# Another order for the steps of the first two of four graph layers: low halves before maxima, joins and statistics

## The chip, the cores and the metric

The kernel runs on one core of a Trainium2 chip. The metric is the time of one execution on the device in microseconds (us), the median of several runs. The two kernels do the same operations on the same tiles; only their order in the engines' queues differs.

## The reference

Four graph layers over 1354 nodes with 256 features, each ahead of a residual sum. `adj` is a sparse weighted 1354 x 1354 matrix.

```python
h = relu(layernorm(x)); x = x + softmax(q k^T / 16 + adj + adj) v            # layer 0: q, k, v = h Wq^T + bq, ...
h = relu(layernorm(x)); x = x + sigmoid(attn_a * x_a + attn_b * x_b)         # layer 1
#   attn_a, attn_b = sigmoid([adj h, h] Wa^T + ba), the same with Wb, bb
#   e = where(adj != 0, exp(-leaky_relu(s_left + s_right^T, 0.01)), 0)
#   x_a = (e h W_sa) / (rowsum(e) + 1e-5);  x_b = adj (h W_gcnb) + b_gcnb
h = relu(layernorm(x)); x = x + (adj != 0) (h W + b) / deg                   # layer 2
h = relu(layernorm(x)); x = x + (S * softmax(mask(h' U h'^T))) h'            # layer 3: h' = h W, S = adj + I
```

## The kernel before

**Tiles.** The node dimension is cut into NB = 11 row blocks of 128 (the last has 74) and NG = 3 column groups: 512, 512 and 330 columns wide, that is 4, 4 and 3 blocks. A tile is one row block by one group, so NT = 33 tiles, n = 11 * group + row block. Tiles 10, 21 and 32 have 74 rows.

**Exactness.** Most products are made of a high and a low half of each operand: hi*hi + hi*lo + lo*hi. ScalarE (ACT) writes the high half, and VectorE (DVE) or GpSimd (POOL) subtracts it from the exact value for the low half. So every sum over a tile (`weighted`, L1508) runs hi matmuls at L1519 and L1520 for each of its blocks, then waits for the low half, then runs the lo matmuls at L1524.

**Order.** Each engine has one queue, whose order is written out by hand, in steps. Between engines there are semaphores only. A wait holds everything that stands behind it on its engine.

**Layer 0, second part** (step `s` from 11 on). TensorE (PE) at step s does `score(s)` (while s < 33) and `aggregate0(s - 15)`, which needs the two exponentials and the low half of tile s - 15. DVE at step s does `add(s)` (L890: scores plus adjacency), `shift(s - 13)` (L929: subtract the maximum), `running(s)` (L921: running maximum over a group) and `weights_lo(s - 14)` (L935: low half of the weights). `add(s)` also waits until `weights_lo(s - 15)` has freed its slot. ACT at step s does `exps(s - 13)`, two exponentials (L523 the high half, L524 the exact value, on which `weights_lo` waits), and up to step 30 one piece of the degree count. `add_out(gi)` (L943, L947) adds a finished group to x on DVE; the next group's first tile waits for it block by block. `top` (L899) turns the maximum of a group into a row: it waits for PE's `turn_max` (which waits for the last `running` of the group), and PE's `spread_max` waits for it. From step 36 on the head of layer 1 is mixed in: `turn(b, 1)` on PE (L1408), `h_full(b)` on ACT (L476), which evacuates it and frees the one bank that all turns use, and the projections `project_g(b)` and `project_h(b)` (L1438). The statistics of the normalisation (`stats` L843, `aggr` L848) are DVE's, and its power and product (`norm`, L376 and L379) are POOL's.

**Layer 1** (step `k` from LEAD = 8 on). PE at step k does `aggregate_b(k)` (adjacency sum, low half `adj_lo(k)`: DVE for even tiles at L1097, POOL for odd ones at L413) and `aggregate_a(k - 8)` (attention sum, low half `e_lo_part(k - 8)`, L1119). Where k is a multiple of 11 the two change places. DVE at step k does `e_lo_part(k - 7)`, a pair `mask` (L1104) and `ramp` (L1112) for a tile ahead of ACT's `exp1` (L643, L644), `adj_lo(k + 1)` where that is even, and once for each group `sums_b` (L1127), `gates`, `join` (L1145 to L1155), `add_gated` (L1163), `stats` and `aggr`. The first tile of a group's `aggregate_a` waits for `join` of the group before, block by block. `ramps_at(k)` (L55) says which ramps stand in a step: one, but two at steps 22 and 27. At steps 14 to 18 DVE also makes masks of layer 2 (`mask_2`, L1174). At steps 34 and 38 PE makes a product of weights (L1415), the second of them after ACT's copy `gram` (L734). ACT's z2 and h2_hi (L482, L490) normalise for layer 2.

## Time and profile before

| | us |
|---|---|
| median of 3 runs | 411.68 |
| the three runs | 411.44, 991.74, 411.68 |
| the profiled execution, its own time | 410.53 |
| its span, from first to last instruction | 408.7 |

The profile is of the execution with 410.53 us, 1.83 us of which lie outside the span. Times of instructions below count from the start of the span. An instruction's row shows when it starts and how long it takes; the next one on an engine may start before it has ended, so the distance of two starts is what a queue pays, and the duration is what a waiter pays. TensorE's granted clock is 0.995 of 2.4 GHz in the mean.

### The profile page before, as it was taken

How to read it: one execution, taken by the hardware profiler on the slowest of the kernel's cores; microseconds unless marked ns; L12 is line 12 of the kernel's file. 1: busy time of each engine (PE TensorE's matmuls, PEld its weight loads, DVE VectorE, ACT ScalarE, POOL GpSimd, SP SyncE). 2: the span in 40 equal slices, each digit the busy share in tenths (PEclk: the TensorE clock that was granted, in tenths of full speed). 3: DMA queues.
4: the chain of work that ended last, by engine and by line, in shares of the span. 5: the costliest groups of instructions: out<-in, count | busy, mean ns of one | idle time of the engine just before them, and what ended most of it. 6: DMA issues, size and time to landing. Idle time of an engine off the chain costs nothing.

```text
span 408.7 us, 7331 instructions
## 1 busy us (share of the span) xinstructions
PE 391.2 (96%) x2526; PEld 353.1 (86%) x2526; DVE 327.6 (80%) x751; ACT 222.7 (54%) x466; POOL 89.7 (22%) x105
## 2 busy tenths in 40 slices
PE   8999999999899999999989999999998999999995
PEld 6788888988899899999989899988887788889863
DVE  6898898899874856998998988765739688798763
ACT  3453798988785657876777891255331312212320
POOL 1290000002010514331130101051010133334552
PEclk9999999999999999999999999999999999999998
DMA  7994000000000001000000000000000000010011
GB/s 233 383 379 142 0 0 2 2 0 2 0 2 0 2 2 51 2 2 0 3 2 0 3 0 2 0 2 2 0 2 0 2 1 0 2 51 2 0 53 33
DMA packets 10317, 13.96 MB, mean 34 GB/s; under 512 B 661, under 2 KB 7209, under 8 KB 10281
## 3 DMA queue, kind: packets, MB, share of 16 engines
q1 hardware_dynamic: 9736, 12.96, 9.3%
q10 hardware_dynamic: 544, 0.52, 0.4%
q8 instruction: 21, 0.34, 0.3%
q14 instruction: 16, 0.12, 0.1%
HBM read 12.10 MB, written 1.39 MB: 33 GB/s over the span
## 4 chain that ended last, share of the span: by engine, by line
PE 77%; DVE 13%; issue 6%; ACT 1%; POOL 1%; DVEq 0%; POOLq 0%; ACTq 0%
PE ps L1805 9%; PE ps L1524 9%; PE ps L1519 8%; PE ps L1520 8%; PE ps L309 8%; PE ps L311 8%; PE ps L310 8%; PE ps L1438 4%; PE ps L1731 3%; PE ps L1732 3%; PE ps L1761 2%; PE ps L1408 2%; DVE m_sb L921 1%; DVE p_lo L935 1%; DVE s_sb L929 1%
## 5 line engine op out<-in xcount | busy, mean ns | idle before, releaser
L1519 PE MATMUL ps<-v_hi,p_hi 128*128 128x258 f32 (+3 forms) x242 | 64.4, 296 | 0.9 <-DVE x_sb L947 0.7
L1520 PE MATMUL ps<-v_lo,p_hi 128*128 128x258 f32 (+3 forms) x242 | 61.1, 281 | 0.0
L1805 PE MATMUL ps<-v,w_ring 128*128 128x256 f32 (+3 forms) x242 | 58.0, 385 | 1.3 <-DVE w_ring L1337 0.8
L1805 PEld LDWEIGHTS ps<-v,w_ring 128*128 128x128 f32 (+3 forms) x242 | 43.2, 186 | 11.0 <-DVE w_ring L1337 4.5
L376 POOL TENSOR_TENSOR mr_all<-mr_all,mhalf 128x4 f32<-128x4 f32 (+1 forms) x12 | 13.3, 1106 | 168.5 <-DVE mr_all L853 168.5
L1519 PEld LDWEIGHTS ps<-v_hi,p_hi 128*128 128x128 f32 (+3 forms) x242 | 44.6, 184 | 2.9 <-ACT p_hi L523 0.9
L814 ACT ACTIVATE s_sb<-s_sb 128x512 f32<-128x512 f32 (+3 forms) x30 | 17.3, 576 | 53.9 <-DVE s_sb L929 53.9
L1520 PEld LDWEIGHTS ps<-v_lo,p_hi 128*128 128x128 f32 (+3 forms) x242 | 44.7, 185 | 0.6
L453 POOL TENSOR_TENSOR total<-total,s_sb 128x512 f32<-128x512 f32 (+3 forms) x27 | 30.6, 1134 | 65.1 <-DVE w_ring L1337 65.1
L1524 PE MATMUL ps<-v_hi,p_lo 128*128 128x258 f32 (+3 forms) x242 | 40.4, 285 | 2.9 <-DVE p_lo L935 2.5
L929 DVE TENSOR_TENSOR s_sb<-s_sb,ps 128x512 f32<-128x512 f32 (+3 forms) x63 | 38.5, 612 | 0.8 <-PE ps L1506 0.7
L1524 PEld LDWEIGHTS ps<-v_hi,p_lo 128*128 128x128 f32 (+3 forms) x242 | 32.5, 185 | 4.3 <-DVE p_lo L935 3.4
L921 DVE TENSOR_TENSOR m_sb<-m_sb,s_sb 128x512 f32<-128x512 f32 (+3 forms) x51 | 33.6, 658 | 0.9
L413 POOL TENSOR_TENSOR mid_lo<-adjT_sb,mid_hi 128x512 fp32r<-128x512 f32 (+2 forms) x16 | 20.6, 1289 | 51.4 <-ACT mid_hi L634 51.4
L1519 PE MATMUL ps<-big_hi,mid_hi 128*128 128x258 f32 (+3 forms) x121 | 31.7, 293 | 0.0
L1520 PE MATMUL ps<-big_lo,mid_hi 128*128 128x258 f32 (+3 forms) x121 | 30.3, 282 | 0.0
L309 PE MATMUL ps<-mid_hi,v_hi 128*128 128x512 f32 (+3 forms) x66 | 28.5, 432 | 1.0 <-DVE v_lo L859 1.0
L643 ACT ACTIVATE p_hi<-s_sb,minus_r 128x512 fp32r<-128x512 f32 (+3 forms) x33 | 22.2, 672 | 11.2 <-PE ps L1524 4.5
L1112 DVE SCALAR_TENSOR_TENSOR s_sb<-s_sb,sx 128x512 f32<-128x512 f32 (+3 forms) x33 | 26.1, 790 | 1.2
L1329 DVE SCALAR_TENSOR_TENSOR s_sb<-adjT_sb,ps 128x512 f32<-128x512 f32 (+3 forms) x30 | 18.5, 616 | 10.0 <-PE ps L311 9.9
L309 PE MATMUL ps<-mid_hi,big_hi 128*128 128x512 f32 (+3 forms) x66 | 25.4, 385 | 0.6 <-DVE mid_lo L872 0.6
L1337 DVE TENSOR_TENSOR w_ring<-s_sb,adjT_sb 128x512 f32<-128x512 f32 (+3 forms) x30 | 19.4, 648 | 7.1 <-ACT s_sb L814 7.1
(228 smaller groups left out, 1045.0 us busy)
## 6 DMA issues: line engine op xcount, KB each, us to landing
adjT_sb<-in_adjT_dram SPq DMA_DIRECT2D x1, 2816.0 KB, 16.7
adjT_sb<-in_adjT_dram SPq DMA_DIRECT2D x3, 768.0 KB, 9.1
adjT_sb<-in_adjT_dram SPq DMA_DIRECT2D x1, 1815.0 KB, 21.2
out_dram<-x_sb SPq DMA_DIRECT2D x10, 128.0 KB
x_sb<-in_x_dram SPq DMA_DIRECT2D x2, 256.0 KB, 3.6
x_sb<-in_x_dram SPq DMA_DIRECT2D x1, 512.0 KB, 4.6
adjT_sb<-in_adjT_dram SPq DMA_DIRECT2D x1, 512.0 KB, 11.4
rows_sb<-in_rows_dram SPq DMA_DIRECT2D x1, 385.0 KB, 11.1
```

The costliest lines, as they stand in the source:

```text
L309: eng.matmul(out_ap, lhs[0], rhs[0], start=first, stop=False)
L310: eng.matmul(out_ap, lhs[0], rhs[1], start=False, stop=False)
L311: return eng.matmul(out_ap, lhs[1], rhs[0], start=False, stop=last)
L453: pool.tensor_tensor(r, r, slot3(n), ALU.add).then_inc(tot_add, 1)
L643: act.activation(ring(p_hi, n), sum1(n), ACT.Exp, bias=bias, scale=SLOPE - 1.0).then_inc(e_hi, 1)
L921: dve.tensor_tensor(m, m, mine(n), op).then_inc(s_max[a], 1)
L929: dve.tensor_tensor(mine(n), mine(n), ps[0:rows(j), bank, 0:CW[gi]], ALU.subtract).then_inc(s_sub[a], 1)
L1112: dve.scalar_tensor_tensor(out=sum1(n), in0=left[0:rows(j), gi, 0:CW[gi]], scalar=sx[0:rows(j), j, 0:1], in1=sum1(n), op0=ALU.add, op1=ALU ...
L1519: pe.matmul(out_ap, left_[0][0:k, n % RING, mine], right_[0][0:k, j, 0:cols_], start=(j == 0), stop=False)
L1520: pe.matmul(out_ap, left_[0][0:k, n % RING, mine], right_[1][0:k, j, 0:cols_], start=False, stop=False)
L1524: ins = pe.matmul(ps[0:rows(b), banks[b % PER], 0:cols_], left_[1][0:k, n % RING, mine], right_[0][0:k, j, 0:cols_], start=False, stop=(j ...
L1805: ins = pe.matmul(ps[0:rows(b), SUMS3[gi][b % PER], 0:D], w_ring[0:k, n % RING, mine], v3[0:k, j, :], start=(j == 0), stop=(j == NB - 1))
```

## The change

All edits are of order.

1. **Layer 0, DVE, steps 14 to 30:** `weights_lo` goes ahead of `add_out` and `running`, and at step 14 ahead of `shift` too.
2. **Layer 0, DVE, steps 31 to 46:** `weights_lo(s - 14)`, then `shift(s - 13)`, now stand before `add(s)`, `add_out` and `running`. The reciprocal of the degrees goes from step 36 to 40.
3. **Layer 0, PE and ACT:** `turn(0, 1)` stands before `aggregate0(21)`, `project_g(0)` before `aggregate0(22)` (it was after `aggregate0(23)`), and ACT's `h_full(0)` a step earlier.
4. **Layer 1, POOL:** `adj_lo(1)` goes ahead of `norm(1, 2)`; `norm(2, 1)` a step later.
5. **Layer 1, DVE:** the double ramp of step 22 goes to step 12, so ramps 8 to 17 come one step sooner. `adj_lo(k + 1)` goes ahead of `join`, `e_lo_part` and the ramps. `add_gated`, `stats` and `aggr` of the first two groups are spread over four steps, two blocks a step.
6. **Layer 1, PE:** `aggregate_b(31)` goes from step 31 to step 30, between `aggregate_b(30)` and `aggregate_a(22)`.

```diff
 def ramps_at(k):
-    first = k - LEAD + 3 + (k > 22) + (k > 27)
-    return range(first, min(first + (2 if k in (22, 27) else 1), NT))
+    first = k - LEAD + 3 + (k > 12) + (k > 27)
+    return range(first, min(first + (2 if k in (12, 27) else 1), NT))
...
             sides(0)
+            adj_lo(1)
             norm(1, 2)
-            adj_lo(1)
             sides(1)
...
-                if k == 35:
+                if k == 36:
                     norm(2, 1)
...
-                if 36 <= s < 40:
+                if s == 35:
+                    h_full(0)
+                if 37 <= s < 40:
                     h_full(s - 36)
...
+                late = s >= NT - 2
+                if late:
+                    weights_lo(s - 14)
+                    if s < NT + 13:
+                        shift(s - 13, 0)
                 if s < NT:
                     add(s)
-                if 13 <= s < NT + 13:
+                if s == 14:
+                    weights_lo(0)
+                if not late and s >= 13:
                     shift(s - 13, 0)
+                if 14 < s < NT - 2:
+                    weights_lo(s - 14)
                 for gi in range(2):
                     if s == NB * gi + 25:
                         add_out(gi)
                 if s < NT:
                     running(s, 0, ALU.max)
-                if s >= 14:
-                    weights_lo(s - 14)
-                if s == 36:
+                if s == 40:
                     dve.wait_ge(nz_sum, NB)
...
                 for gi in range(NG):
                     if k == NB * gi + 11:
                         sums_b(gi)
-                    if gi < 2 and k == NB * gi + 19:
+                if k + 1 < NT and (k + 1) % 2 == 0:
+                    adj_lo(k + 1)
+                for gi in range(2):
+                    if k == NB * gi + 19:
                         join(gi)
                 if m + 1 < NT:
                     e_lo_part(m + 1)
                 for n in ramps_at(k):
                     mask(n)
                     ramp(n)
-                if k + 1 < NT and (k + 1) % 2 == 0:
-                    adj_lo(k + 1)
...
-                    if gi < 2 and k == NB * gi + 21:
-                        add_gated(gi)
-                    if gi < 2 and k == NB * gi + 22:
-                        for b in blocks(gi):
-                            stats(b, 2)
-                    if gi < 2 and k == NB * gi + 23:
-                        for b in blocks(gi):
-                            aggr(b, 2)
+                for gi in range(2):
+                    b0, step = blocks(gi)[0], k - NB * gi - 21
+                    if step in (0, 1):
+                        add_gated(b0 + 2 * step)
+                        add_gated(b0 + 2 * step + 1)
+                    if step in (1, 2):
+                        stats(b0 + 2 * step - 2, 2)
+                        stats(b0 + 2 * step - 1, 2)
+                    if step in (2, 3):
+                        aggr(b0 + 2 * step - 4, 2)
+                        aggr(b0 + 2 * step - 3, 2)
...
+                if s == 36:
+                    pe.wait_ge(s_sub[0], 2 * NB)
+                    turn(0, 1)
+                if s == 37:
+                    project_g(0)
                 if s >= LAG:
                     aggregate0(s - LAG)
...
-                if s == 36:
-                    pe.wait_ge(s_sub[0], 2 * NB)
-                if 36 <= s < 40:
+                if 37 <= s < 40:
                     turn(s - 36, 1)
-                if 38 <= s < 42:
+                if 39 <= s < 42:
                     project_g(s - 38)
...
-                if k < NT and k % NB:
+                if k < NT and k % NB and k != 31:
                     aggregate_b(k)
+                if k == 30:
+                    aggregate_b(31)
                 aggregate_a(k - LEAD)
```

`add_gated` now takes a block in place of a group; the last group's call loops over its blocks.

## Rows read from the trace of the kernel before

**Rows 1.** The page, busy time of each engine over the span.

```profile
PE 391.2 (96%) x2526; PEld 353.1 (86%) x2526; DVE 327.6 (80%) x751; ACT 222.7 (54%) x466; POOL 89.7 (22%) x105
```

**Rows 2.** Windows: stretch, its length, each engine's busy us, clock, DMA.

```profile
100.00:110.00 10.00, 8.37 (x66) 7.65 (x64) 8.77 (x20) 7.17 (x15) 2.23 (x2) 1.00 0.00 1
...
230.00:240.00 10.00, 9.39 (x63) 8.28 (x63) 8.11 (x31) 10.00 (x24) 1.42 (x2) 1.00 0.01 3
```

**Rows 3.** Waits of PE over the span: total us, times, longest.

```profile
PE ps L1524 <- DVE p_lo L935: 2.5, 4, 1.0
...
PE ps L1524 <- DVE p_lo L1119: 0.4, 2, 0.2
```

**Rows 4.** Timeline, step 14 of layer 0: start, duration, engine, line.

```profile
52.02 0.62 ACT L524 ACTIVATE s_sb<-s_sb 128x512 f32<-128x512 f32 x1
...
52.57 0.68 DVE L929 TENSOR_TENSOR s_sb<-s_sb,ps 128x512 f32<-128x512 f32 x1
...
53.77 0.69 DVE L935 TENSOR_TENSOR p_lo<-s_sb,p_hi 128x512 fp32r<-128x512 f32 x1
...
54.51 0.76 PE L1524 MATMUL ps<-v_hi,p_lo 128*128 128x258 f32 x4 [0.72 <-DVE p_lo L935]
```

**Rows 5.** Timeline, step 25 of layer 0.

```profile
82.82 1.66 DVE L947 SCALAR_TENSOR_TENSOR x_sb<-ps,rinv,x_sb 128x256 f32<-128x256 f32 x4
...
84.39 0.49 DVE L921 TENSOR_TENSOR m_sb<-m_sb,s_sb 128x330 f32<-128x330 f32 x1
...
85.54 0.76 PE L1524 MATMUL ps<-v_hi,p_lo 128*128 128x258 f32 x4 [0.50 <-DVE p_lo L935]
```

**Rows 6.** Timeline, steps 32 to 37 of layer 0.

```profile
102.18 0.67 DVE L929 TENSOR_TENSOR s_sb<-s_sb,ps 128x512 f32<-128x512 f32 x1
...
102.31 0.75 PE L1524 MATMUL ps<-v_hi,p_lo 128*128 128x258 f32 x4 [0.96 <-DVE p_lo L935]
...
103.43 0.61 ACT L524 ACTIVATE s_sb<-s_sb 128x512 f32<-128x512 f32 x1
...
104.20 0.64 PE L1524 MATMUL ps<-v_hi,p_lo 128*128 128x258 f32 x4
...
108.06 0.18 DVE L943 RECIPROCAL rinv<-ps 128x4 f32<-128x4 f32 x1 [0.77 <-PE ps L1524]
108.17 0.46 ACT L524 ACTIVATE s_sb<-s_sb 128x330 f32<-128x330 f32 x1
...
108.92 0.36 PE L1519 MATMUL ps<-v_hi,p_hi 128*128 128x258 f32 x1 [0.67 <-DVE x_sb L947]
```

**Rows 7.** Timeline, start of layer 1's sums.

```profile
137.68 1.55 POOL L376 TENSOR_TENSOR mr_all<-mr_all,mhalf 128x3 f32<-128x3 f32 x1 [4.29 <-DVE mr_all L853]
...
140.00 1.53 POOL L413 TENSOR_TENSOR mid_lo<-adjT_sb,mid_hi 128x512 fp32r<-128x512 f32 x1
...
141.58 0.75 PE L1524 MATMUL ps<-big_hi,mid_lo 128*128 128x258 f32 x4 [0.96 <-POOL mid_lo L413]
...
142.17 0.38 PE L1408 MATMUL ps<-ident,z_buf 128*128 128x128 f32 x2
```

**Rows 8.** Timeline, steps 8 to 30 of layer 1.

```profile
157.62 0.42 DVE L1104 TENSOR_SCALAR s_sb<-adjT_sb 128x512 f32<-128x512 f32 x1
...
160.59 1.29 POOL L413 TENSOR_TENSOR mid_lo<-adjT_sb,mid_hi 128x512 fp32r<-128x512 f32 x1 [0.81 <-ACT mid_hi L634]
...
160.63 1.54 DVE L1104 TENSOR_SCALAR s_sb<-adjT_sb 128x512 f32<-128x512 f32 x1
...
188.76 0.16 DVE L1145 TENSOR_TENSOR rs<-ps,e_left 128x4 f32<-128x4 f32 x1 [0.98 <-PE ps L1524]
...
193.41 0.74 PE L1524 MATMUL ps<-big_hi,mid_lo 128*128 128x258 f32 x4 [0.38 <-DVE mid_lo L1097]
...
205.59 0.62 PE L1524 MATMUL ps<-big_hi,mid_lo 128*128 128x258 f32 x3 [1.41 <-DVE mid_lo L1097]
...
221.59 0.36 PE L1519 MATMUL ps<-v_hi,p_hi 128*128 128x258 f32 x1 [0.21 <-DVE s_sb L1155]
```

More of the change, by code:

```diff
@@ L1156, in join, with add_gated @@
                                              op1=ALU.add).then_inc(joined, 1)
-            def add_gated(gi):
-                for b in blocks(gi):
-                    r = rows(b)
-                    dve.wait_ge(th_set, b + 1)
-                    dve.scalar_tensor_tensor(out=x_sb[0:r, b, :], in0=t2[0:r, gi % 2, b % PER, :], scalar=0.5,
-                                             in1=x_sb[0:r, b, :], op0=ALU.mult, op1=ALU.add).then_inc(x_add[1], 1)
+            def add_gated(b):
+                r, gi = rows(b), b // PER
+                dve.wait_ge(th_set, b + 1)
+                dve.scalar_tensor_tensor(out=x_sb[0:r, b, :], in0=t2[0:r, gi % 2, b % PER, :], scalar=0.5,
+                                         in1=x_sb[0:r, b, :], op0=ALU.mult, op1=ALU.add).then_inc(x_add[1], 1)
             def mask_2(n):
@@ L1238, in _ @@
                         gates(gi)
-                    if gi < 2 and k == NB * gi + 21:
-                        add_gated(gi)
-                    if gi < 2 and k == NB * gi + 22:
-                        for b in blocks(gi):
-                            stats(b, 2)
-                    if gi < 2 and k == NB * gi + 23:
-                        for b in blocks(gi):
-                            aggr(b, 2)
+                for gi in range(2):
[9 more added lines that the diff above has]
+                        aggr(b0 + 2 * step - 3, 2)
                 if 14 <= k < 19:
@@ L1285, in _ @@
                 mask_2(n)
-            add_gated(2)
+            for b in blocks(2):
+                add_gated(b)
             for b in blocks(2):
```

## The prediction

> **What bounds the kernel now.** I read the page's busy times first. PE works 391.2 of 408.7 us [rows 1], so an edit of order can give back only what PE waits. Then the waits of PE by releaser: nearly all inside the first two layers are waits of a sum's lo matmuls (L1524) for a low half on another engine, 2.5 us for `weights_lo` and 0.4 for `e_lo_part` [rows 3], and single ones for `adj_lo`, the longest 1.41 [rows 8]. Then the windows: the worst stretch is 100 to 110, the end of layer 0, with PE at 8.37 of 10 and DVE at 8.77, while 230 to 240, the end of layer 1, has PE at 9.39 and ACT at 10.00 [rows 2]. Last the timeline at each wait [rows 4 to 8], for what stood on the late engine ahead of the thing waited for. No queue of DMA is in any of these chains.
>
> **Layer 0, step 14.** The exact value of tile 0 is there at 52.64 (52.02 + 0.62). DVE does `shift(1)` at 52.57, a `running` after it, and `weights_lo(0)` only at 53.77: two operations at 0.60 each ahead of it. PE starts the lo matmuls at 54.51 after 0.72 idle [rows 4]. In the new order `weights_lo(0)` starts at about 52.70 and ends at 53.39, before PE wants it, and the restart costs PE another 0.1 (its group takes 0.76 where an undelayed one takes 0.64 [rows 4, 6]). Saved: 1.0 with the end of the previous matmul counted in. `shift(1)` is 0.7 later, but PE needs its tile two us after that. Bounds: 0.7 to 1.0.
>
> **Layer 0, step 25.** Four `add_out` operations start at 82.82 and take 1.66, `running` follows at 84.39, `weights_lo(11)` behind it, and PE stands until 85.54 after 0.50 idle [rows 5]. With `weights_lo(11)` first, it ends before `add_out` starts. `add_out` itself then comes 0.24 later relative to PE, because the low half takes 0.60 of a 0.36 us gap, and PE's hi matmuls follow it block by block. Saved: 0.50 + 0.1 of restart + 0.2 of end overlap, less 0.24, about 0.55. Bounds 0.3 to 0.8.
>
> **Layer 0, steps 31 to 46: here I expect a loss.** At step 32 the new order cures the longest wait for a `weights_lo`, 0.96 at 102.31 [rows 6]. But `weights_lo(n)` ahead of `shift(n + 1)` joins two engines in one chain: `shift(n)` 0.67, two exponentials until 1.19 after the shift's end (shift at 102.18 + 0.67 = 102.85, second exponential ends at 103.43 + 0.61 = 104.04 [rows 6]), `weights_lo(n)` at 0.60, then the next shift. That is 0.67 + 1.19 + 0.04 + 0.60 = 2.50 a tile. Before, `shift(n + 1)` went out while ACT still worked on tile n, and the pair cost DVE 1.2. PE needs 12 matmuls at 0.12, that is 1.43, for a tile of the second group (0.12 is from the undelayed group of four at 104.20: 0.64 less 0.28, over 3). Nothing else stands in DVE's steps 33 and 35 to fill the gap. From the two-operation chain of step 32 I count on, in the present clock less the 1.5 gained so far:
> - `running(32)` is now behind `weights_lo`, `shift` and `add`: `turn_max` waits 0.7, `spread_max` 0.6.
> - `weights_lo` of tiles 19, 20 and 21 go out 2.5 apart: the sum of tile 21 waits 0.4 for its hi and 0.3 for its lo half.
> - `add_out(1)` starts 0.7 later than the present 108.06, at 108.8. PE meets `project_g(0)`, whose `h_full(0)` stands on ACT behind the exponentials of tile 22: 1.4 of wait.
> - `turn(2)` and `turn(3)` need one bank that `h_full` frees, behind exponentials that come later: 0.4 and 0.5.
>
> Together 4.3 of waits in place of the present 0.96 + 0.67 [rows 6] + 0.7 in three short ones around tile 22, which is 2.3: a loss of 2.0. From step 39 on each step has 0.9 us of projection in it, PE's step is about 2.0, and the chain for a 330-wide tile (0.41 + 0.5 + 0.83 + waits, the two exponentials from 0.37 and 0.46 [rows 6]) is about 1.9, so nothing more is lost. Moving `turn(0)` and `project_g(0)` puts 0.25 and 0.7 us of PE work into these waits; without it the loss would be larger by as much. Bounds: a gain of 1.6, if all the old waits go and none comes, to a loss of 6, if steps 39 to 46 lose 0.5 each.
>
> **Layer 1, POOL.** `norm(1, 2)` takes POOL from 137.68 to 140.00, `adj_lo(1)` ends at 141.53, PE stands 0.96 and turns block 8 at 142.17 [rows 7]. The new `adj_lo(1)` can start at 137.1 and ends by 138.6 at the latest. `norm` then ends 0.5 to 1.0 after the present 140.00, and z(8) with it, so the turn is what is late next: it comes at 141.4 to 141.7 where it would be free at 140.94. Saved 0.7; bounds 0.4 and 1.2.
>
> **Layer 1, steps 12 to 22.** The extra `mask` and `ramp` cost DVE 1.12 at step 12. The one long idle of DVE that can take it is the 0.98 before `join(0)` [rows 8]; small ones on the way I put at 0.5 together. `adj_lo(20)`, now ahead of `join(0)`, wants 0.60 of the same 0.98. So `join(0)` comes up to 0.5 late, and the sum behind it too, while PE's wait of 0.38 before 193.41 for `adj_lo(20)` [rows 8] goes, with 0.1 of restart. Net 0.2 saved, bounds from a loss of 0.6 to a gain of 0.6.
>
> **Layer 1, steps 22 to 24.** PE stands 1.41 before 205.59 for `adj_lo(24)` [rows 8], behind two ramp pairs, four gated sums and four statistics. Of these one ramp pair (1.12), two gated sums and two statistics go elsewhere, and `adj_lo` moves ahead of `e_lo_part` and a ramp (1.7). It can then start near 201.3 and PE wants it at 204.2. Saved: 1.41 + 0.1 = 1.5; bounds 1.0 and 1.5.
>
> **Layer 1, steps 30 to 37.** `aggregate_b(31)` fills the wait for `join(1)`: 0.21 [rows 8], 0.1 of restart and 0.2 of pacing block by block, 0.5. Its own low half has been ready for 4 us. The two waits for `e_lo_part` (0.4, [rows 3]) lose most of their cause: 0.3. Bounds 0.2 and 1.1 for both.
>
> **Rules weighed.** A mask of DVE takes 1.54 at 160.63, beside POOL's subtraction of 160.59 [rows 8]; alone, at 157.62, it takes 0.42 [rows 8]. The Trainium skill says why (SBUF — State Buffer, section "Who interferes with whom"): DVE and GpSimd share a pair of ports as an exclusive lock for a whole instruction. By that rule the extra mask of step 12 may meet a POOL subtraction, which is rival R5 below; the trace agrees with it at 160.63.
>
> **The sum.** -1.0 - 0.55 + 2.0 - 0.7 - 0.2 - 1.5 - 0.5 - 0.3 = -2.75. On the profiled execution, 410.53, that gives 407.8. The median of the runs shown is 1.15 above that execution, so the same difference gives 408.9 against 411.68. A measurement of this kernel can tell about 2%, or 8 us, from no change.
>
> **The rivals** (times on the median's scale).
> - *R1, the late steps cost nothing.* For it: ACT is busy only 7.17 of 10 in that stretch [rows 2] and PE has other work moved in. Against: a semaphore chain doesn't care how busy its engines are. 408.9 - 2.0 = 406.9.
> - *R2, the late steps gain all they can.* The 1.6 instead of the loss of 2.0: 405.3.
> - *R3, layer 1's gains are given back.* ACT is full from 230 to 240 [rows 2]. If its work, not its start, sets the end of layer 1, the 2.5 us of steps 12 to 37 go: 411.4. Against: its stretch starts with `sums_b(2)`, which also comes earlier.
> - *R4, slower.* The chain of `shift`, exponentials and `weights_lo` doesn't end at step 38 but also sets steps 39 to 46, because ACT has `h_full`, `h1_hi` and `z` in its queue between two tiles. Eight steps at 0.5 are 4.0 more: 412.9. It decides from the point at which the chain is longer than PE's step of 2.0; my 1.9 is close below.
> - *R5, the shared operands.* The mask and ramp of step 12 meet POOL's subtraction and take 1.1 more, `join(0)` is 1.0 later still and PE with it: 409.9.
> - *R6, no effect.* Freed waits reappear at once behind the same DVE, which is full for most of both layers: 411.7.
>
> **Chances.** Forecast 0.42, R1 0.19, R2 0.05, R3 0.14, R4 0.08, R5 0.06, R6 0.06. The forecast's own range is 407.4 to 410.4; with the rivals and the bounds 405.4 to 412.3. No case reaches 8 us either way, so within 2% has 0.95; PE's whole idle is 408.7 - 391.2 = 17.5 us [rows 1], of which start, end and two more layers take a share; so faster by over 2% has 0.03 and slower 0.02.
>
> **What would show it.** Right: no PE wait near 54 and 85; the long one at 102 gone, but new ones at `spread_max`, at `project_g(0)` and at the turns after it; `weights_lo` operations of tiles 19 to 21 about 2.5 apart; no PE wait of 1.4 for `adj_lo(24)`; a wait of about 0.5 before the turn of block 8. From the start of score step 31 to the first sum of layer 1 PE takes about 2 us more than now, and from there to 240 about 3 less. Wrong: if PE passes the end of layer 0 sooner by more than 1 us, the chain wasn't binding; if PE waits at steps 39 to 46, R4; if the second layer is no shorter, R3 or R6.

## The result, and the profile after

The changed kernel takes 409.7 us (median of 9 runs, 409.23 to 410.7), the kernel before, run beside it, 411.65. The ratio is 0.9971 with a 95% interval of 0.9958 to 0.9983: 1.2 us less (0.7 to 1.7), where 2.75 were predicted. The two medians lie 1.95 apart; the ratio leaves out two of the nine executions of the kernel before, of 646.73 and 991.74 us. The time is inside the predicted range, the size of the effect is not what was worked out.

The profiled execution took 410.70 us against 410.53 before, 0.17 more. Its first `add` of layer 0 starts at 18.78, before at 17.66. That is 1.12 us more of start-up, ahead of all that was changed, and the start varies between 17.65 and 18.71 in the experiments below. So I compare from that `add` on. Call L the time from it to the last group of lo matmuls of layer 1's sums: 222.67 us before (17.66 to 240.33), 221.73 after (18.78 to 240.51), 0.94 less. Each kernel has one trace. Where two kernels do the same, the distances between groups of matmuls mostly repeat to 0.02 us, so L can be read stretch by stretch. Three places repeat less well: the end of layer 0 when the clock falls there (0.1), the third tile of layer 1 (0.08), and the group of `adj_lo(26)` (up to 0.3, see E12).

The windows of the changed kernel that answer to [rows 2], with six single microseconds between them (stretch, length, busy us of PE, PEld, DVE, ACT and POOL, PE's granted clock, DMA):

```profile
100.00:110.00 10.00, 7.71 (x58) 6.64 (x56) 7.13 (x15) 6.04 (x12) 0.78 (x2) 1.00 0.00 1
230.00:240.00 10.00, 8.91 (x61) 8.02 (x60) 8.53 (x33) 9.81 (x23) 1.44 (x2) 1.00 0.01 3
109.00:110.00 1.00, 0.05 (x1) 0.05 (x1) 0.82 (x2) 0.90 (x3) 0.00 (x0) 1.00 0.00 0
110.00:111.00 1.00, 1.00 (x3) 0.83 (x4) 0.96 (x4) 0.88 (x3) 0.00 (x0) 0.61 0.00 0
111.00:112.00 1.00, 1.00 (x4) 0.81 (x4) 1.00 (x4) 0.46 (x1) 0.00 (x0) 0.50 0.00 0
112.00:113.00 1.00, 1.00 (x7) 1.00 (x6) 1.00 (x4) 0.28 (x1) 0.00 (x0) 0.50 0.00 0
113.00:114.00 1.00, 1.00 (x8) 1.00 (x8) 1.00 (x4) 0.57 (x2) 0.00 (x0) 0.69 0.00 0
114.00:115.00 1.00, 1.00 (x11) 1.00 (x11) 1.00 (x7) 0.94 (x3) 0.00 (x0) 1.00 0.00 0
```

The end of layer 0 has become worse (PE 7.71 of 10, it was 8.37), and after a microsecond with next to nothing on PE its clock goes from 2.4 to 1.2 GHz and is back at 1.00 only from 114 on. The end of layer 1 is worse too (8.91, it was 9.39; the windows are fixed in time and this trace starts 1.12 later, so they don't hold quite the same work).

The waits of PE by line, the five largest behind that `add` and inside the first two layers (in all, times, longest; one of the two for `m_sb`, of 0.2, lies in a later layer):

```profile
PE ps L1451 <- ACT h_mid L476: 1.3, 1, 1.3
PE ps L1532 <- DVE s_sb L1164: 1.2, 1, 1.2
PE ps L1537 <- DVE p_lo L1128: 1.1, 2, 0.6
PE ps L1510 <- DVE m_sb L923: 0.6, 2, 0.4
PE ps L1519 <- DVE mx L909: 0.4, 1, 0.4
```

L1451 is `project_g`, L1532 the hi matmuls behind `join`, L1537 the lo matmuls, L1510 and L1519 `turn_max` and `spread_max`. The 2.5 us for `weights_lo` of [rows 3] are gone altogether. Of these five, those of `project_g` and `spread_max` are new. The wait behind `join` was 0.2 (behind `join(1)`), those for `e_lo_part` 0.4, and `turn_max` had none in these layers and now has 0.43.

**The two cured waits.** The timeline at step 14 and step 25, DVE then PE:

```profile
53.80 0.69 DVE L937 TENSOR_TENSOR p_lo<-s_sb,p_hi 128x512 fp32r<-128x512 f32 x1
54.41 0.68 DVE L931 TENSOR_TENSOR s_sb<-s_sb,ps 128x512 f32<-128x512 f32 x1
54.77 0.64 PE L1537 MATMUL ps<-v_hi,p_lo 128*128 128x258 f32 x4
...
82.46 0.68 DVE L937 TENSOR_TENSOR p_lo<-s_sb,p_hi 128x512 fp32r<-128x512 f32 x1
83.27 1.66 DVE L949 SCALAR_TENSOR_TENSOR x_sb<-ps,rinv,x_sb 128x256 f32<-128x256 f32 x4
```

The low half now goes ahead of the shift and of `add_out`, and the PE row at 54.77 has no bracket, so no wait. Against [rows 4, 5] PE is 0.91 and 0.55 sooner at the groups that follow, once the 1.12 are taken off. At step 25 a wait of 0.21 stays, for `add_out`, as worked out (0.24).

**The chain at the end of layer 0.** The timeline of DVE's low halves and of PE there:

```profile
102.16 0.69 DVE L937 TENSOR_TENSOR p_lo<-s_sb,p_hi 128x512 fp32r<-128x512 f32 x1 [0.28 <-ACT s_sb L524]
104.66 0.69 DVE L937 TENSOR_TENSOR p_lo<-s_sb,p_hi 128x512 fp32r<-128x512 f32 x1 [0.35 <-ACT s_sb L524]
107.17 0.69 DVE L937 TENSOR_TENSOR p_lo<-s_sb,p_hi 74x512 fp32r<-74x512 f32 x1 [1.22 <-ACT s_sb L524]
109.95 1.87 PE L1451 MATMUL ps<-raw_b,h_mid 128*128 128x258 f32 x4 [1.30 <-ACT h_mid L476]
```

The low halves are 2.50 us apart, as worked out, each after DVE sat idle until ScalarE's second exponential (the brackets), and `project_g(0)` waits 1.30 (1.4 predicted).

**Around `join(0)`.** POOL, DVE and PE:

```profile
189.56 1.28 POOL L413 TENSOR_TENSOR mid_lo<-adjT_sb,mid_hi 75x512 fp32r<-75x512 f32 x1 [4.21 <-ACT mid_hi L636]
189.59 1.52 DVE L1182 TENSOR_SCALAR spare_mask<-adjT_sb 128x512 fp32r<-128x512 f32 x1
191.04 0.68 DVE L1106 TENSOR_TENSOR mid_lo<-adjT_sb,mid_hi 128x512 fp32r<-128x512 f32 x1
191.64 0.15 DVE L1154 TENSOR_TENSOR rs<-ps,e_left 128x4 f32<-128x4 f32 x1
192.87 0.36 PE L1532 MATMUL ps<-v_hi,p_hi 128*128 128x258 f32 x1 [1.16 <-DVE s_sb L1164]
```

A mask of 0.42 takes 1.52 beside POOL's subtraction for tile 21, `adj_lo(20)` follows, and only then `join(0)` begins. Before, DVE had 0.98 of idle there [rows 8]. That idle is gone.

The steps of the prediction against the two traces (distance between groups of lo matmuls, after less before):

| term | predicted | measured |
|---|---|---|
| layer 0, step 14 | -1.0 | -0.91 |
| layer 0, step 25 | -0.55 | -0.55 |
| layer 0, steps 31 to 46 | +2.0 | +2.17 |
| layer 1, POOL's order | -0.7 | -0.33 |
| layer 1, steps 12 to 22 (`join(0)`) | -0.2 | +0.70 |
| layer 1, steps 22 to 24 (`adj_lo(24)`) | -1.5 | -1.67 |
| layer 1, steps 30 to 37 | -0.5 - 0.3 | -0.31 |
| sum | -2.75 | -0.90, of L's -0.94 |

### The profile page after: what moved, and what is told of

The parts are those of the page before. It is cut to its first block, busy times and chain, and to the rows that moved or that the text cites. A ratio compares the mean times of both kernels' runs of the same rounds, so it can differ in the third digit from the quotient of the medians.

```text
span 408.9 us, 7331 instructions
## 1 busy us (share of the span) xinstructions
PE 393.3 (96%) x2526; PEld 355.2 (87%) x2526; DVE 329.8 (81%) x751; ACT 222.4 (54%) x466; POOL 90.1 (22%) x105
## 4 chain that ended last, share of the span: by engine, by line
PE 80%; DVE 11%; issue 5%; ACT 2%; DVEq 0%; POOLq 0%; POOL 0%; ACTq 0%
PE ps L1823 9%; PE ps L309 8%; PE ps L311 8%; PE ps L310 8%; PE ps L1532 8%; PE ps L1537 8%; PE ps L1533 8%; PE ps L1451 4%; PE ps L1750 3%; PE ps L1749 3%; PE ps L1779 2%; PE ps L1421 2%; DVE p_lo L1128 2%; DVE s_sb L931 1%; PE ps L1556 1%
## 5 line engine op out<-in xcount | busy, mean ns | idle before, releaser
L1532 PE MATMUL ps<-v_hi,p_hi 128*128 128x258 f32 (+3 forms) x242 | 64.7, 298 | 1.5 <-DVE s_sb L1164 1.2
L1532 PEld LDWEIGHTS ps<-v_hi,p_hi 128*128 128x128 f32 (+3 forms) x242 | 45.0, 186 | 3.3 <-issue 1.8
L1537 PE MATMUL ps<-v_hi,p_lo 128*128 128x258 f32 (+3 forms) x242 | 40.5, 285 | 1.1 <-DVE p_lo L1128 1.1
L1537 PEld LDWEIGHTS ps<-v_hi,p_lo 128*128 128x128 f32 (+3 forms) x242 | 32.8, 186 | 1.8 <-DVE p_lo L1128 1.6
L1532 PE MATMUL ps<-big_hi,mid_hi 128*128 128x258 f32 (+3 forms) x121 | 31.7, 293 | 0.0
L937 DVE TENSOR_TENSOR p_lo<-s_sb,p_hi 128x512 fp32r<-128x512 f32 (+3 forms) x33 | 20.6, 623 | 6.2 <-ACT s_sb L524 5.9
```

What stands on the lines that cost most here:

```text
L1532: pe.matmul(out_ap, left_[0][0:k, n % RING, mine], right_[0][0:k, j, 0:cols_], start=(j == 0), stop=False)
L1537: ins = pe.matmul(ps[0:rows(b), banks[b % PER], 0:cols_], left_[1][0:k, n % RING, mine], right_[0][0:k, j, 0:cols_], start=False, stop=(j ...
```

## The experiments

Each kernel was timed beside the kernel before. E1 to E4, E5 to E8 and E9 to E12 ran together, with a median of before of 411.05, 411.35 and 411.0, where it was 411.65 beside the changed kernel. So medians from different groups can differ by some tenths for no reason of the kernels. There the ratios, each to its own kernel before, are the better measure, and for small effects L. L is as above.

| run | median us | ratio to before, 95% | L |
|---|---|---|---|
| changed kernel | 409.7 | 0.9971 (0.9958, 0.9983) | 221.73 |
| E1 late order off | 406.5 | 0.9897 (0.988, 0.9913) | 218.35 |
| E2 mask behind join | 409.95 | 0.9969 (0.9959, 0.998) | 221.20 |
| E3 group 2 whole | 410.42 | 0.9988 (0.9977, 0.9999) | 221.96 |
| E4 PE kept busy | 409.35 | 0.9967 (0.9954, 0.9979) | 221.33 |
| E5 PE's and ACT's moves back | 411.76 | 1.0009 (0.9997, 1.0021) | 223.28 |
| E6 E1 and E5 together | 406.44 | 0.9882 (0.9867, 0.9898) | 218.53 |
| E7 E1, ramp back at 22 | 405.26 | 0.9856 (0.9842, 0.987) | 216.95 |
| E8 E1, POOL's order back | 407.04 | 0.99 (0.9886, 0.9914) | 218.75 |
| E9 E1, small subtraction | 405.9 | 0.9872 (0.9856, 0.9887) | 217.45 |
| E10 E1, join first | 406.48 | 0.9892 (0.9877, 0.9906) | 218.23 |
| E11 before, steps 14 to 30 alone | 409.41 | 0.9957 (0.9941, 0.9973) | 220.98 |
| E12 E7, aggregates later | 405.69 | 0.9866 (0.9848, 0.9884) | 217.21 |

**E1: the late order off.**

```diff
-                late = s >= NT - 2
+                late = False
...
-                if not late and s >= 13:
+                if 13 <= s < NT + 13:
                     shift(s - 13, 0)
-                if 14 < s < NT - 2:
+                if 14 < s:
                     weights_lo(s - 14)
```

> The changed kernel with only VectorE's order of steps 31 to 46 put back (shift before weights_lo; the moved turn and projection of TensorE, the moved h_full of ScalarE and all of the rest stay). Theory (the chain weights_lo, shift, two exponentials, 2.5 us a tile, is what costs): the stretch from score step 31 to the first sum of layer 1 is 1.5 to 2.5 us shorter than in the changed kernel, the old wait of about 1 us for a low half near 101 is back, the granted clock stays at 1.00 in 110 to 114; about 407.7 against 409.7. Rival (the moved turn and projection, or h_full a step earlier, cost the time): no shorter by more than 0.5 us, the clock still falls.

3.2 us less by the medians (3.0 by the ratios), 3.38 in L, nearly all of it (3.31) between step 31 and the end of layer 0. The theory holds and the size is larger than the bound given: the old wait doesn't come back as 1 us but as 0.27, since `weights_lo` still stands ahead of `running`. E1's windows:

```profile
100.00:110.00 10.00, 9.60 (x73) 8.87 (x73) 9.38 (x22) 8.08 (x18) 0.62 (x1) 1.00 0.00 0
110.00:120.00 10.00, 9.79 (x67) 8.83 (x66) 8.50 (x27) 8.69 (x25) 1.44 (x2) 1.00 0.01 2
```

**E5 and E6: the moved turn, projection and `h_full` put back,** with the late order (E5) and without it (E6).

```diff
-                if s == 35:
-                    h_full(0)
-                if 37 <= s < 40:
+                if 36 <= s < 40:
...
-                if s == 36:
-                    pe.wait_ge(s_sub[0], 2 * NB)
-                    turn(0, 1)
-                if s == 37:
-                    project_g(0)
...
-                if 37 <= s < 40:
+                if s == 36:
+                    pe.wait_ge(s_sub[0], 2 * NB)
+                if 36 <= s < 40:
                     turn(s - 36, 1)
-                if 39 <= s < 42:
+                if 38 <= s < 42:
                     project_g(s - 38)
```

> The changed kernel with the moved turn(0), project_g(0) and h_full(0) put back in their old steps; VectorE's late order stays. Theory of the prediction (the moved work fills waits that the chain of 2.5 us a tile makes): without it the end of layer 0 is 0.5 to 0.9 us longer, about 410.4. Rival (project_g(0) comes where its h_full isn't done, stands 1.3 us and brings the clock down, and that is what costs): the stretch is 0.5 us or more shorter and the clock stays at 1.00 in 110 to 114; about 409.0 or less.

> As the kernel with VectorE's late order undone (406.5), with turn(0), project_g(0) and h_full(0) put back too. Where the late order alone costs the 3.3 us, this one is within 0.5 us of 406.5, a little slower since the move fills the wait at spread_max: about 406.9. Rival (the order and the move are only bad together): it is as fast as 406.5 and the kernel with the move alone undone is as fast too.

E5 is 2.1 us slower than the changed kernel by the medians (1.6 by the ratios, 1.55 in L), E6 the same as E1. So the move is worth nothing by itself and about 1.6 us under the late order. The rival falls: PE without the moved work waits longer, 1.97 for `add_out(1)`, and its clock stays down longer. The row and the windows of E5:

```profile
109.93 0.55 PE L1530 MATMUL ps<-v_hi,p_hi 128*128 128x258 f32 x1 [1.97 <-DVE x_sb L947]
```

```profile
108.00:109.00 1.00, 0.00 (x0) 0.00 (x0) 0.74 (x2) 0.72 (x2) 0.00 (x0) 0.72 0.00 0
109.00:110.00 1.00, 0.07 (x1) 0.10 (x1) 0.96 (x4) 0.80 (x3) 0.00 (x0) 0.50 0.00 0
...
115.00:116.00 1.00, 1.00 (x5) 0.82 (x5) 0.88 (x2) 0.38 (x1) 0.92 (x2) 0.86 0.00 0
```

Against the kernel before, the stretch from step 31 to the last sum of layer 0 is 2.17 longer in the changed kernel, 3.86 in E5, 1.13 shorter in E1 and 0.97 in E6.

**E4: PE kept busy in the wait.** `idle(1, 3)` issues three matmuls whose result nobody reads.

```diff
                 if s == 37:
+                    idle(1, 3)
                     project_g(0)
```

> The changed kernel with three matmuls more of 256 columns into a bank that nobody reads, ahead of the moved projection, in the wait of 1.3 us in which TensorE's granted clock goes from 1.00 to 0.50. They compute nothing that is used. Theory (it is this wait that brings the clock down, and the clock's fall costs about 1 us of matmuls at double length between 110 and 113.6): the clock stays at 1.00 there and the kernel takes 0.7 to 1.2 us less: about 408.7. Rival (what follows waits for VectorE and ScalarE in any case, so slower matmuls only fill waits): the clock stays up, and waits of 0.3 to 0.5 us for turn(2) and turn(3) show in place of the slower matmuls; within 0.3 us of the changed kernel.

0.35 us less by the medians, 0.40 in L, between theory and rival; the intervals of the ratios overlap. The clock stays up, and PE then waits for the turns (0.7 in two waits for `h_mid`, the 0.4 and 0.5 that the prediction had there). The 0.40 is not a firm price of the clock. E2 and E3 below have the changed kernel's order up to here, and their clock falls too, but they enter layer 1's sums (tile 5) 0.25 and 0.18 ahead of it in L, and E4 0.39: against them E4 saves only 0.14 and 0.21. The times point to more. In three of the changed kernel's nine executions the mean granted clock is 0.996 or 0.997, as in all five of E4 (0.996 to 0.998), and they take 409.23 to 409.42 us; the six with 0.993 or 0.994 take 409.65 to 410.70, in the median 0.8 more. It may be that the clock didn't fall in those three. None of them has a trace, and the start-up can differ as well, so this is not shown. E4's windows:

```profile
110.00:111.00 1.00, 1.00 (x9) 0.91 (x8) 1.00 (x3) 0.30 (x1) 0.00 (x0) 1.00 0.00 0
111.00:112.00 1.00, 1.00 (x11) 1.00 (x10) 1.00 (x4) 0.44 (x2) 0.00 (x0) 1.00 0.00 0
```

**E2: one mask moved behind `join(0)`.**

```diff
-                if 14 <= k < 19:
+                if 14 <= k < 18:
                     mask_2(k - 14)
+                if k == 19:
+                    mask_2(4)
```

> The changed kernel with one mask (the fifth mask of the second kind) moved from step 18 to step 19, behind join(0), so that VectorE doesn't run it beside GpSimd's subtraction for tile 21. Theory (the collision of the two, 1.52 instead of 0.42 us, makes join(0) late): the wait of 1.16 us ahead of the sum behind join(0) falls to 0.2 or less, and the kernel takes 0.8 to 1.1 us less: about 408.8. Rival (adj_lo(20) ahead of join(0), 0.60 us, is what makes it late): the mask's own 0.42 at most is saved, under 0.5 us. Third: the mask meets another subtraction in its new place, and the time moves on by as much: no gain.

L is 0.53 shorter, which the medians and the overlapping intervals don't show. Only 0.34 of that is the edit's, at the wait behind the join, which falls from 1.16 to 0.82; 0.25 was there before it (E3, without this edit, has 0.18 of them). The third case comes nearest, in another way than written: the moved mask meets nothing, but POOL's subtraction now meets `adj_lo(20)`, and that takes 1.78 in place of 0.68.

```profile
188.82 1.27 POOL L413 TENSOR_TENSOR mid_lo<-adjT_sb,mid_hi 75x512 fp32r<-75x512 f32 x1 [4.21 <-ACT mid_hi L636]
188.86 1.78 DVE L1106 TENSOR_TENSOR mid_lo<-adjT_sb,mid_hi 128x512 fp32r<-128x512 f32 x1
```

**E9: the subtraction itself made small.** On top of E1, POOL's `adj_lo(21)` works on 8 of 512 columns; the rest of that low half is left out.

```diff
+                w = 8 if n == 21 else CW[n // NB]
-                pool.tensor_tensor(adj_ring(at[1], n), adj_tile_b(n), f(adj_ring(at[0], n)), ALU.subtract).then_inc(alo_odd, 1)
+                pool.tensor_tensor(adj_ring(at[1], n)[:, 0:w], adj_tile_b(n)[:, 0:w], f(adj_ring(at[0], n))[:, 0:w],
+                                   ALU.subtract).then_inc(alo_odd, 1)
```

> As the kernel with VectorE's late order undone (406.5), with GpSimd's subtraction for tile 21 of layer 1 done on 8 of its 512 columns (the low half of that tile is left out but for these). Theory (that subtraction stretches VectorE's mask from 0.42 to 1.52 us, and this is 1.1 of the lateness of join(0)): the mask takes 0.42 again, join(0) and the matmuls behind it come 1.0 to 1.1 us sooner, about 405.5. Rival (join(0) is late by VectorE's queue, the extra mask and ramp and adj_lo(20), and would be late without the collision): under 0.3 us saved, 406.2 or more.

The mask takes 0.44, PE's wait behind the join is gone, and the next group comes 1.08 sooner than in E1. By the medians 0.6 is saved, by the ratios 1.0, in L 0.90 (E9's trace had lost 0.16 ahead of this place). The 1.08 are the collision's price at this place. Without the collision the sum behind `join(0)` is still 0.26 later than in the kernel before, counted from the sums ahead of it: that is what DVE's fuller queue costs.

```profile
185.71 0.20 POOL L414 TENSOR_TENSOR mid_lo<-adjT_sb,mid_hi 75x8 fp32r<-75x8 f32 x1 [4.21 <-ACT mid_hi L638]
185.75 0.44 DVE L1184 TENSOR_SCALAR spare_mask<-adjT_sb 128x512 fp32r<-128x512 f32 x1
```

**E10: `join(0)` ahead of `adj_lo(20)`,** on top of E1.

```diff
-                if k + 1 < NT and (k + 1) % 2 == 0:
+                if k != 19 and k + 1 < NT and (k + 1) % 2 == 0:
                     adj_lo(k + 1)
                 for gi in range(2):
                     if k == NB * gi + 19:
                         join(gi)
+                if k == 19:
+                    adj_lo(k + 1)
```

> As the kernel with VectorE's late order undone (406.5), with join(0) ahead of adj_lo(20) at step 19, as before the change. Theory (0.60 us of join(0)'s lateness is adj_lo(20) ahead of it, but PE needs adj_lo(20) next): the wait of 1.16 us behind join(0) falls to about 0.6, and a wait of 0.4 to 0.6 for adj_lo(20) comes back: within 0.2 us of 406.5. Rival (adj_lo(20) ahead is a plain loss): 0.5 to 0.6 us saved, about 405.9.

No change (406.48). The join's wait falls to 0.56 and PE gains 0.60 there, and all but 0.12 of L goes again. It isn't a wait for `adj_lo(20)` that takes it back, as I expected, but small steps later on, 0.28 of them near the group of `adj_lo(26)`. E12 has a like step there (0.31), with an edit that can't have caused it, so how much of the 0.60 the order itself takes back stays open.

**E7: the doubled mask and ramp back at step 22,** on top of E1.

```diff
-    first = k - LEAD + 3 + (k > 12) + (k > 27)
-    return range(first, min(first + (2 if k in (12, 27) else 1), NT))
+    first = k - LEAD + 3 + (k > 22) + (k > 27)
+    return range(first, min(first + (2 if k in (22, 27) else 1), NT))
```

> As the kernel with VectorE's late order undone (406.5), with the doubled mask and ramp at step 22 again instead of step 12 (adj_lo stays ahead). Theory (the extra 1.1 us of VectorE at step 12 is what makes join(0) late; the subtraction of GpSimd takes its 1.1 us wherever it falls): the wait of 1.16 us behind join(0) is gone or under 0.3, and adj_lo(24), which is ahead of its step's ramp now, still comes with 0.5 us of wait or less; 0.5 to 1.1 us saved, about 405.7. Rival (the doubled ramp at 22 brings the old wait of 1.4 us for adj_lo(24) back): the one gain pays for the other, 406.3 to 406.8.

1.2 us less than E1 by the medians (1.7 by the ratios), 1.40 in L, more than the 0.5 to 1.1 of the theory. PE no longer waits behind `join(0)`, nor for `adj_lo(24)`. So the ramp's move isn't what cures that wait; which of the rest does, `adj_lo` ahead of the ramps or the spread gated sums and statistics, was not tried apart. E7 has the lowest median here, 405.26 us, below the kernel before and the changed one by more than the intervals. Its DVE and POOL at the join:

```profile
183.86 0.42 DVE L1182 TENSOR_SCALAR spare_mask<-adjT_sb 128x512 fp32r<-128x512 f32 x1
184.19 0.68 DVE L1106 TENSOR_TENSOR mid_lo<-adjT_sb,mid_hi 128x512 fp32r<-128x512 f32 x1
185.12 1.28 POOL L413 TENSOR_TENSOR mid_lo<-adjT_sb,mid_hi 75x512 fp32r<-75x512 f32 x1 [3.80 <-ACT mid_hi L636]
185.85 0.16 DVE L1154 TENSOR_TENSOR rs<-ps,e_left 128x4 f32<-128x4 f32 x1 [0.98 <-PE ps L1537]
```

The subtraction starts in DVE's idle of 0.98, as it did before the change. So the theory was wrong in one point: the subtraction doesn't take its 1.1 us wherever it falls.

**E8: POOL's order back,** on top of E1.

```diff
+            norm(1, 2)
             adj_lo(1)
-            norm(1, 2)
```

> As the kernel with VectorE's late order undone (406.5), with norm(1, 2) of GpSimd ahead of adj_lo(1) again. Theory (the swap saved 0.33 us by the trace, not the 0.7 predicted, because the turn of block 8 waits for z behind the later norm): the first sums of layer 1 come 0.2 to 0.5 us later, about 406.85. Rival (with the end of layer 0 shorter and PE less behind, the swap gains nothing): within 0.1 us of 406.5.

0.5 us more by the medians, 0.1 by the ratios, whose intervals overlap, and 0.40 in L. The swap saves 0.4 by the traces; the times don't settle it.

**E3: the second group's gated sums, statistics and aggregates whole.**

```diff
+                if k == NB + 21:
+                    for b in blocks(1):
+                        add_gated(b)
+                if k == NB + 22:
+                    for b in blocks(1):
+                        stats(b, 2)
+                if k == NB + 23:
+                    for b in blocks(1):
+                        aggr(b, 2)
-                for gi in range(2):
+                for gi in range(1):
```

> The changed kernel with the gated sums, statistics and aggregates of the second group (steps 32 to 34) done whole, one kind a step, as before; the first group's stay two a step. Theory (two statistics and two aggregates now stand ahead of the last low halves): the two waits of TensorE near 233 and 235 (0.5 and 0.6 us) shrink to the old 0.2 and 0.2, and 0.4 to 0.7 us are saved: about 409.2. Rival (what follows is bound by ScalarE, full from 230 to 240): the waits shrink and the time stays as it is, within 0.2 us.

The sign is wrong: 0.7 us slower by the medians, with intervals that overlap, and 0.23 in L. The trace was 0.18 ahead when it came to the edit, so the edit costs 0.42. The two waits do shrink, to 0.25 and 0.20. But four gated sums at once hold up what follows on DVE: PE stands 0.46 for a low half at 228.83, and `zz`, for which ScalarE waits, starts 209.69 after the first `add` in E3 (228.00 less 18.31) and 209.21 after it in the changed kernel (227.99 less 18.78), so 0.48 later. From `zz` on E3's ScalarE has no gap that the waits list, so that start probably sets the end.

```profile
228.00 0.16 DVE L1136 TENSOR_TENSOR zz<-ps,sx 128x6 f32<-128x6 f32 x1
228.83 0.62 PE L1546 MATMUL ps<-v_hi,p_lo 128*128 128x258 f32 x3 [0.46 <-DVE p_lo L1128]
233.20 0.62 PE L1546 MATMUL ps<-v_hi,p_lo 128*128 128x258 f32 x3 [0.25 <-DVE p_lo L1128]
```

**E12: the second group's aggregates a step later,** on top of E7.

```diff
-                    if step in (2, 3):
-                        aggr(b0 + 2 * step - 4, 2)
-                        aggr(b0 + 2 * step - 3, 2)
+                    late_2 = step - gi
+                    if late_2 in (2, 3):
+                        aggr(b0 + 2 * late_2 - 4, 2)
+                        aggr(b0 + 2 * late_2 - 3, 2)
```

> The best so far (VectorE's late order undone, doubled ramp at step 22: 405.3), with the aggregates of the second group one step later, behind the low halves that PE waits for near 228 and 230 (0.48 and 0.61 us). Theory (these waits come of what stands ahead of e_lo_part): they fall to 0.2 to 0.3 each; ScalarE is full behind them, so of the 0.5 us that PE wins only 0.1 to 0.3 reach the end: about 405.1. Rival (PE sets the end there): 0.5 us less, 404.8.

No gain: the intervals of E7 and E12 overlap, and L is 0.26 longer. The two waits fall from 0.48 and 0.60 to 0.36 and 0.32. Of the 0.40 that PE wins there it loses 0.29 over the groups that follow. Another 0.31 goes near the group of `adj_lo(26)`, ahead of anything this edit touches. The trace shows where: beside a subtraction of POOL, two gated sums of DVE take 1.35 together, because the second, from 198.65 on, takes 1.02 in place of 0.42.

```profile
198.32 1.35 DVE L1171 SCALAR_TENSOR_TENSOR x_sb<-s_sb,x_sb 128x256 f32<-128x256 f32 x2
198.62 0.77 POOL L413 TENSOR_TENSOR mid_lo<-adjT_sb,mid_hi 128x330 fp32r<-128x330 f32 x1 [4.57 <-ACT mid_hi L636]
```

In E7 the second gated sum starts at 198.26, 0.02 behind POOL's 198.24, but there DVE's pair takes 0.75 (from 197.93) and POOL pays, 1.08 for 0.77. Hundredths decide who pays, finer than these rows can tell who came first. A difference of 0.3 between two single traces can be no more than that.

**E11: steps 14 to 30 alone,** on the kernel before.

```diff
+                if s == 14:
+                    weights_lo(0)
                 if 13 <= s < NT + 13:
                     shift(s - 13, 0)
+                if 14 < s < NT - 2:
+                    weights_lo(s - 14)
...
-                if s >= 14:
+                if s >= NT - 2:
                     weights_lo(s - 14)
```

> The kernel before with one part of the change alone: weights_lo ahead of shift at step 14 and ahead of add_out and running in steps 15 to 30; steps 31 on and all of the rest as before. Theory (these two waits were PE's own and nothing takes it back): 1.45 to 1.6 us less than before, about 409.8 against 411.4. Rival (a part is given back at steps 31 to 38, where VectorE is late in any case): 0.5 to 1.0 us less.

1.6 us less by the medians, 1.69 in L, 0.28 of it at the wait of step 32, which shrinks from 0.96 to 0.69. Nothing is given back: by itself this part takes more off L than the whole change (1.69 against 0.94).

## Why the prediction was right and wrong

**Steps 14 and 25** came out as worked out (-0.91 and -0.55 for -1.0 and -0.55), and E11 shows that they stay.

**Steps 31 to 46** lost 2.17 for 2.0, with the chain that was worked out: low halves 2.50 apart, a wait of 1.30 at `project_g(0)`. R1 and R2 fall, and so does R4, as no wait of PE is listed at the steps from 39 on. R6 falls by the interval. But that the sum agrees so well is luck. The prediction had 4.3 us of waits in place of 2.3. In the stretch from the group ahead of step 32's to the last of layer 0 (99.75 to 132.90 before, 99.42 to 134.75 after) PE is idle for 1.97 before, since the three short waits put at 0.7 are one of 0.34, and for 2.29 after: `turn_max` and `spread_max` wait 0.43 each for 0.7 and 0.6, nothing of tile 21 waits longer than 0.11, and the waits for the turns (0.4 and 0.5) don't show. The rest of the loss is longer matmuls, 33.04 us of PE busy for 31.18, at a mean clock of 0.95 in that stretch. With the clock kept up (E4) 1.87 of the 2.17 stay all the same: the added matmuls fill the wait of 1.30, and PE is idle for another 1.70, of which 0.35 and 0.34 for the turns. I also gave the PE moves their 0.95 us of filled waits; under this order they are worth 1.7 (E5's stretch less the changed kernel's), since without them the clock is down longer too. The larger miss is what I did not ask: what the same stretch would do with the early steps' order. E1 shows 1.13 less than before, so the late order costs 3.3, not 2.

**Steps 12 to 22 is the step that failed**: +0.70 for -0.2, with 0.9 us the largest error. I charged the mask and ramp and `adj_lo(20)` to DVE's idle of 0.98 ahead of `join(0)` and allowed for 0.5 of lateness, and that part held: without the collision it is 0.26 (E9). What I put at nothing is POOL's subtraction for tile 21, which lay in the same idle: in the trace of before it starts 0.73 ahead of DVE's 188.76 [rows 8], where DVE is idle:

```profile
188.03 1.28 POOL L413 TENSOR_TENSOR mid_lo<-adjT_sb,mid_hi 75x512 fp32r<-75x512 f32 x1 [3.79 <-ACT mid_hi L634]
```

With DVE later, the two run at once, and E9 prices that at 1.08. The 1.34 by which the sum behind `join(0)` comes late are these 1.08 and the 0.26; the wait for `adj_lo(20)` that goes and its restart give back 0.63. This is R5's mechanism, with its price (1.0) right and its place wrong: not the mask of step 12 but one that wasn't moved, six steps on. It had a chance of 0.06. At this place DVE alone pays, 0.42 to 1.52 and 0.68 to 1.78, while POOL's 1.28 and 1.27, begun just ahead of DVE's, are what they are with DVE idle (1.28 in E7). Elsewhere POOL pays too. In the changed kernel its subtraction of 128x512 takes 1.09 alone, and 1.84 where an operation of DVE began 0.06 ahead of it and kept its usual 0.75:

```profile
154.80 1.09 POOL L413 TENSOR_TENSOR mid_lo<-adjT_sb,mid_hi 128x512 fp32r<-128x512 f32 x1 [2.99 <-ACT mid_hi L636]
168.08 0.75 DVE L1121 SCALAR_TENSOR_TENSOR s_sb<-s_sb,sx 128x512 f32<-128x512 f32 x1
168.14 1.84 POOL L413 TENSOR_TENSOR mid_lo<-adjT_sb,mid_hi 128x512 fp32r<-128x512 f32 x1 [4.20 <-ACT mid_hi L636]
```

The Trainium skill (SBUF — State Buffer, section "Who interferes with whom") says that whoever comes first holds the shared ports for its whole instruction and the other blocks. By that rule the first of the two keeps its time and the second pays, and these rows agree, as far as two starts a few hundredths apart can be told in them.

**Steps 22 to 24**: -1.67 for -1.5. But I credited the ramp's move with part of it, and E7 shows that the gain stays without the move. So the edit that brought the collision about was not needed for this wait.

**POOL's order**: -0.33 for -0.7 (E8: 0.4). The turn of block 8 stands at 143.29, and PE entered the stretch 1.85 late, so it came at 141.44 on before's scale, inside the predicted 141.4 to 141.7, though without the wait that I expected ahead of it. Of that gain of 0.73, 0.66 is left at tile 2's lo matmuls and 0.33 at tile 3's. Between these stand the next block's turn and projection, behind an `h_full` of ScalarE, and ScalarE had come to `z` 0.5 later against the start of the stretch. I had not priced that. Also unpriced is a DVE operation of 0.17 that takes 0.90 beside the moved `adj_lo(1)` and holds `adj_lo(0)`:

```profile
138.98 1.09 POOL L413 TENSOR_TENSOR mid_lo<-adjT_sb,mid_hi 128x512 fp32r<-128x512 f32 x1 [3.75 <-ACT mid_hi L636]
139.20 0.90 DVE L854 TENSOR_SCALAR mr_all<-mr_all 128x3 f32<-128x3 f32 x1
140.81 0.74 PE L1537 MATMUL ps<-big_hi,mid_lo 128*128 128x258 f32 x4 [0.20 <-DVE mid_lo L1106]
```

**Steps 30 to 37**: -0.31 for -0.8. `aggregate_b(31)` gave 0.64, more than its 0.5. But the two waits for `e_lo_part`, of which I had 0.3 going, grew from 0.20 each to 0.48 and 0.61. Two statistics and two aggregates now stand ahead of the first low half, two aggregates and the two operations that finish them ahead of the second. That costs 0.69; with another 0.05 lost ahead of them, 0.41 comes back right behind. R3 falls: ScalarE's full stretch starts 210.58 after the first `add` before (228.24 less 17.66) and 209.40 after (228.18 less 18.78), 1.18 sooner, with PE 1.27 sooner there, so nearly all that was gained ahead of it reaches it, as the prediction said. That ScalarE's work then limits what PE can win behind it is argued, not shown; E3 and E12 agree with it.

The errors of three steps, 0.9 at 12 to 22, 0.37 at POOL's order and 0.49 at 30 to 37, and 0.09 less at step 14, 0.17 more at the late steps and 0.17 less at `adj_lo(24)` together make the 1.85 between -2.75 and -0.90.

## What to carry to other kernels

An engine's idle time in a trace isn't free room: before spending it, look at what the engine that it collides with does in it. When work is put ahead of other work so that its consumer waits less, check that the operation now behind it doesn't feed the same producer: low half before shift cured one wait and tied DVE and ScalarE into a chain of 2.5 us a tile, which cost 3.3. And price each part of a change against the same change without it, not against the kernel before; here the late order cost 3.3 and the ramp's move 1.3 us, and the projection's move only repaired a part of the first.

## What was not expected of the hardware

**TensorE's clock in a short wait.** The granted clock went from 2.4 to 1.2 GHz around a wait of 1.30 us, in a stretch with PE at 7.71 of 10, and took until 114 to come back with PE always busy. In E2 and E3 it fell inside that same wait (0.62 and 0.63 in the microsecond from 109). In the trace of before it stayed at 1.00 in that stretch with PE at 8.37 of 10 and no wait above 0.96. The matmuls of a sum took 0.42 (at 111.83) in place of 0.28 (at 113.93). The four windows from 110 to 114 lack 0.39 + 0.50 + 0.50 + 0.31 = 1.70 us of full clock, and keeping the clock up saved 0.40 in L, or 0.14 to 0.21 against E2 and E3. The Trainium skill (TensorE: Matmul & The Clock Gate, section "Terms") puts the penalty at about the time at the lower clock times the share of pulses lost. By that rule the estimate is those 1.70. In the traces it is an upper bound here, since most of the slow matmuls lay where PE would have waited, as E4 shows.

**The collision moves, it doesn't go.** In E2, E9 and E7 the same POOL operation cost DVE 1.10 on a subtraction, next to nothing when it was small (0.44 for 0.42), and nothing when it fell into an idle of DVE.
